# Spreading the softmax reciprocals over the channels: a float32 product of four rows becomes a float16 product of eight rows

## What is computed

```
qkv = (xs @ w_proj.T + b_proj).reshape(B, H * W, N_HEADS, 3 * D_K)
q, k, v = split(qkv)                        # 4 heads, D_K = 16, 784 tokens
attn = softmax(einsum('bihk,bjhk->bijh', q, k) * D_K**0.5, axis=2)
h = einsum('bjhk,bijh->bihk', v, attn)      # weighted values
h = h.reshape(B, H*W, 64) @ w_out.T + b_out
h = h * sigmoid(h) + xs
```

## Time and profile before

| what | value |
|---|---|
| median of 3 runs | 1832.68 us (1827.34 to 1839.15) |
| the profiled execution, its own time | 1829.92 us |
| its span, first to last instruction | 1828.1 us |
| mean granted clock of TensorE | 0.949 of full speed |
| PE busy | 1663.0 us, 91% of the span |
| DVE busy | 1285.1 us, 70% |
| ACT busy | 1022.2 us, 56% |
| POOL busy | 434.1 us, 24% |
| share of PE in the chain that ended last | 81% |

### The profile page before, as it was taken

How to read it: one execution, slowest core, us unless ns; L and a number is a source line. 1 busy time by engine, 2 the same in 40 slices (tenths; PEclk the granted TensorE clock), 3 DMA queues, 4 the chain that set the end, 5 groups by cost and what they waited for, 6 DMA issues and landing times.

```text
span 1828.1 us, 35089 instructions
## 1 busy us (share of the span) xinstructions
PE 1663.0 (91%) x10910; PEld 751.8 (41%) x10910; DVE 1285.1 (70%) x2603; ACT 1022.2 (56%) x1401; POOL 434.1 (24%) x333
## 2 busy tenths in 40 slices
PE   0799689997884999999999999999999999999997
PEld 0333245554873244444434434434443443444332
DVE  5677467887784887777767767666776776767762
ACT  0100166674331176777767667666676776767676
POOL 0400011112102212423413223232341423323111
PEclk9999899999897599999999989989999999999999
DMA  8111166663002332332233322332322332224300
GB/s 197 41 51 45 40 108 100 109 102 54 0 0 33 50 43 33 48 58 43 35 48 50 49 43 33 47 51 46 48 33 43 53 53 43 33 47 54 47 11 19
DMA packets 70267, 93.31 MB, mean 51 GB/s; under 512 B 22648, under 2 KB 63224, under 8 KB 69968
## 3 DMA queue, kind: packets, MB, share of 16 engines
q1 hardware_dynamic: 67728, 89.59, 29.9%
q0 software_dynamic: 2368, 1.57, 1.0%
HBM read 9.00 MB, written 6.42 MB: 8 GB/s over the span
## 4 chain that ended last, share of the span: by engine, by line
PE 81%; DVE 6%; ACT 4%; DMA 3%; SPq 3%; issue 3%; DVEq 0%; POOL 0%; ACTq 0%; POOLq 0%
PE ps L1051 20%; PE ps L1041 18%; PE ps L986 16%; PE ps L861 8%; PE ps L885 5%; PE ps L900 3%; PE ps L1032 3%; PE ps L1007 2%; ACT arena L679 2%; DMA x<-x_in 2%; PE ps L947 2%; SPq L433 2%; PE ps L1024 1%; DVE arena L1430 1%; PE ps L1015 1%
## 5 line engine op out<-in xcount | busy, mean ns | idle before, releaser
L1430 DVE TENSOR_REDUCE arena<-ps 128x1 f32<-128x392 f32 x1600 | 827.0, 559 | 329.5 <-PE ps L986 316.1
L792 ACT ACTIVATE arena<-ps 112x784 f32<-112x784 f32 x896 | 703.4, 822 | 270.4 <-PE ps L1041 265.8
L986 PE MATMUL ps<-arena 112*128 112x392 bf16 x1536 | 491.1, 348 | 8.7 <-DMA arena<-arena 8.2
L1041 PE MATMUL ps<-arena 114*112 114x392 bf16 x1792 | 457.1, 342 | 19.9 <-issue 14.8
L1051 PE MATMUL ps<-arena 112*32 112x392 f32 x3584 | 401.2, 520 | 0.4 <-ACT arena L792 0.4
L986 PEld LDWEIGHTS ps<-arena 112*128 112x128 bf16 x1536 | 151.2, 99 | 377.4 <-DVE arena L1430 307.5
L1041 PEld LDWEIGHTS ps<-arena 114*112 114x112 bf16 x1792 | 230.2, 136 | 140.7 <-issue 50.8
L885 PE MATMUL ps<-arena 96*128 96x392 f16 x768 | 142.2, 336 | 22.0 <-DMA arena<-arena 16.5
L679 ACT ACTIVATE arena<-ps,magic,arena 128x784 f32<-128x784 f32 x128 | 128.2, 1004 | 37.2 <-PE ps L885 37.0
L861 PE MATMUL ps<-arena 128*64 128x392 f32 (+1 forms) x768 | 139.5, 505 | 3.9 <-DMA arena<-arena 3.9
L1051 PEld LDWEIGHTS ps<-arena 112*32 112x32 f32 x3584 | 71.3, 109 | 147.7 <-issue 146.0
(11 more groups left out here) (139 smaller groups left out, 1381.9 us busy)
## 6 DMA issues: line engine op xcount, KB each, us to landing
arena<-arena SPq DMA_DIRECT2D x504, 73.5 KB, 2.7
arena<-arena SPq DMA_DIRECT2D x256, 84.2 KB, 2.8
x<-x_in SPq DMA_DIRECT2D x8, 784.0 KB, 21.2
out<-x SPq DMA_DIRECT2D x16, 392.0 KB, 2.4
arena<-arena SPq DMA_DIRECT2D x252, 24.5 KB, 2.3
arena<-arena SPq DMA_DIRECT2D x256, 1.5 KB
arena<-arena SPq DMA_DIRECT2D x16, 225.0 KB, 3.4
arena<-arena SPq DMA_DIRECT2D x16, 224.8 KB, 2.9
```

Of the source, the lines that this page charges most:

```text
L792: nc.scalar.activation(probs[w % 2][:, 2 * pair:2 * pair + 2, :], two(2 * place, rows=slice(0, TT)), ACT.Exp).then_inc(s_taken, 1)
L986: last = nc.tensor.matmul(ps[:, bank, 0:CH], q[0:ROWS_L, h, it * 128:(it + 1) * 128], k[0:ROWS_L, h, c * CH:(c + 1) * CH], start=True, sto ...
L1041: last = nc.tensor.matmul(ps[0:TT, 2 * place + j, 0:CH], ks[s % 4][0:ROWS_ALL, h, jt * TT:(jt + 1) * TT], qs[s % 4][0:ROWS_ALL, h, c * CH: ...
L1430: nc.vector.tensor_reduce(mx[img % 2][:, c, v:v + 1], scores, AX.X, ALU.max).then_inc(s_mf, 1)
```

## The change

DVE makes two float16 numbers of every reciprocal, times 1024: the rounded value, and what the rounding left. `gather` sends them as two transfers to eight rows. The stationary matrix becomes 8 x 128 float16 with entries 1/1024, so that the product adds the high and the low part again. It is cast once, ahead of the attention's first token.

```diff
+RECIP_UNIT = 1024.0
...
-        den_row = part([NH, T])
+        den_parts = part([NH * DEN_ROWS, 2, T // DEN_ROWS], F16)
+        den_row = part([2 * NH, T], F16)
+        head_rows = part([2 * NH, 128], F16)
...
             def gather(n):
                 wait_apart(pool, s_recip, n)
-                pool.dma_start(den_row[:, :], den_packed[:, :]).then_inc(s_row, 16)
+                for k in range(2):
+                    pool.dma_start(den_row[k * NH:(k + 1) * NH, :], den_parts[:, k, :]).then_inc(s_row, 16)
...
-                    last = nc.tensor.matmul(ps[:, 2 * place + c, 0:CH], P("head_rows", NH),
+                    last = nc.tensor.matmul(ps[:, 2 * place + c, 0:CH], head_rows[:, :],
                                             den_row[:, c * CH:(c + 1) * CH], start=True, stop=True)
...
                     if what == "den":
-                        pe.wait_ge(s_row, lin(lambda t: 16 * t, s, i, 4))
+                        pe.wait_ge(s_row, lin(lambda t: 32 * t, s, i, 4))
...
             v.tensor_scalar(q_bias[:, :], P("bq"), DK**0.5, None, ALU.mult)
+            link(v.tensor_copy(head_rows[:, :], P("head_rows", 2 * NH)))
...
             def reciprocals(n16):
                 dve.wait_ge(s_packed, n16)
-                v.reciprocal(den_packed[:, :], den_packed[:, :]).then_inc(s_recip, 1)
+                link(v.reciprocal(den_packed[:, :], den_packed[:, :]))
+                link(v.tensor_scalar(den_parts[:, 0, :], den_packed[:, :], RECIP_UNIT, None, ALU.mult))
+                v.scalar_tensor_tensor(den_parts[:, 1, :], den_packed[:, :], RECIP_UNIT, den_parts[:, 0, :],
+                                       ALU.mult, ALU.subtract).then_inc(s_recip, 1)
```

More of the change, by code:

```diff
@@ L1504, in _ @@
             v.tensor_tensor(xp(NP - 1), xp(NP - 1), gate[:, :], ALU.add).then_inc(s_done, 1)
-LINKS3 = 4 * 1
+LINKS3 = 4 * 3
 def pack(a):
@@ L1556, in pack @@
     put("b_out", np.tile(a["L3_conv_b_out"], 2)[:, None])
-    put("head_rows", np.kron(np.eye(NH, dtype=f), np.ones((1, 2 * DK), f)), slice(0, NH))
+    rows = np.kron(np.eye(NH, dtype=f), np.full((1, 2 * DK), 1.0 / RECIP_UNIT, f))
+    put("head_rows", np.concatenate([rows, rows]), slice(0, 2 * NH))
     w0 = a["L0_conv_weight"].transpose(1, 0, 3, 4, 2).reshape(C, W0_COLS)
```

## The result

The changed kernel takes 1788.4 us (median of 4 runs, 1786.88 to 1790.92), the kernel before 1833.28 us in the same comparison (4 runs, 1827.34 to 1839.15): 0.976 times as long, 95% interval 0.972 to 0.979. The profiled execution took 1786.88 us at a mean granted clock of 0.963. Against the 1829.92 us of the profiled execution before that is 43.0 us less; 44.1 less were forecast (1785.8, given as 1786 us).

The account below looks back on a forecast made before the run. PE's queue was taken to bound the attention, with low-clock stretches behind "den" adding time. 1829.9 - 23.0 (queue) - 21.4 (clock) + 0.3 = 1785.8, given as 1786 us; range 1773 to 1812 us.

Parts of the forecast that it names:

- the queue of the attention: PE's work and waits around "den": 0.85 us less in 15 even steps, 0.64 in 16 odd ones, together 23.0 us.
- the clock: 17 stretches of PE at 1.2 GHz behind "den" go, 1.26 us each, 21.4 us; bounds nothing and 29 us.
- ahead of the attention's first reciprocal: One chained cast of the matrix ahead of the first token: 0.2 us, taken as 0.25.
- The exponential's wait: The unit after "den" needs the place ACT's exponential frees, so starts at least 1.47 us after the unit before.
- The pitch of the product: On PE the float16 "den" product was taken at 0.17 us, one instruction each; float32 cost 1.56 us extra per entry.
- The 0.04 us: Gain per entry because the first score product behind a float32 one takes 0.21 us to its second instead of 0.17.
- DVE's chain: Three small DVE instructions make reductions 0.5 us later, delaying PE 0.5 us in odd steps and 0.28 in even ones.
- The gather: POOL's second transfer, issued 0.70 us later, makes PE wait 0.45 us in even steps, covered by the exponential; none in odd.
- The 1.26 us: Price of one low-clock stretch, from differences between loop rounds of 149.33, 152.95 and 154.58 us.
- the clock stays: Rival: the low-clock stretches have another cause or the new idle time brings them too; 1807 us, chance 0.19.
- The gather's second transfer sets the start of "den": Rival: 4.0 us from issue to landing; even steps lose 0.53 us, odd ones stay; 1817 us, chance 0.11.
- run one behind the other: Rival: the gather's two transfers are serial, the second there 5.68 us after the first issue; 1861 us, chance 0.04.

Follow-up runs that it names:

- experiment 2: Kernel before with the float16 product of four rows and one transfer, the low part of the reciprocals left out: 1775.58 us, ratio 0.968.
- experiment 5: Changed kernel with its float16 product over 128 rows, the 120 added ones holding ones with zero weights: 1785.8 us, ratio 0.976.
- experiment 3: Kernel before with its float32 product over 128 rows instead of four, the added rows meeting zero weights: 1791.49 us, ratio 0.977.
- experiment 6: Changed kernel with the output store of odd steps issued ahead of the 24 copies of q and k: 1783.77 us, ratio 0.974.
- experiment 4: Changed kernel with each float16 product of eight rows issued five times: 1877.24 us, ratio 1.022 to the kernel before.
- experiment 1: Kernel before, float32 product kept, plus the two chained DVE instructions and a second transfer that PE waits for: 1852.62 us, ratio 1.008.
- experiment 11: Changed kernel, store first, odd-step "den" behind unit 25 instead of 24, odd-step reciprocals at unit 20 instead of 18: 1792.16 us, ratio 0.976.

## Why the prediction was right

The mechanism held: the queue on PE sets the pace, the exponential of the unit before sets what an entry can gain, and the 17 stretches at 0.50 go. That the total came so close (1785.8 us forecast, 1786.88 in the profiled execution, 1788.4 the median) is luck, for its terms were off by more, in both directions. From one profiled execution to the other, read off the timelines:

| part | forecast, us | measured, us |
|---|---|---|
| the queue of the attention | -23.0 | -16.5 |
| the clock | -21.4 | -29.5 |
| ahead of the attention's first reciprocal | +0.3 | +3.2 |
| idle in the gaps between rounds | 0 | -0.3 |
| sum | -44.1 | -43.1 |

**The queue.** The entries are 27.2 us shorter from unit to unit. From the reciprocal to the unit of "den" the steps are 10.7 us longer, 7.6 in odd and 3.1 in even ones. That leaves 16.5 us: 9.3 in odd steps, where 10.2 were forecast, and 7.2 in even ones, where 12.8 were. The missing part is the gather.
- *The exponential's wait* held to 0.02 us: 1.49 us in odd steps and in unhindered even ones, against 1.47 forecast. It stays at 1.49 with one transfer (experiment 2) and with 128 rows (experiment 5).
- *The pitch of the product* was mis-sized: 0.27 us where 0.17 was taken from the wide float16 products of the second layer. It cost nothing, as experiment 5 shows, because the exponential ends later. What the prediction charged to the float32 form (1.56 us for an entry) is in part a matter of four rows: 0.58 us (experiment 3).
- *The 0.04 us* for a faster pair of score products behind "den" did not come: the pair still shows 0.54 us. It was 1.2 us of the 23.0.
- *DVE's chain* was right: 0.67 us to the next reduction against 0.24 before, so 0.43 us where 0.5 was forecast, and it reaches PE as 0.51 us in odd steps and 0.21 in even ones, where 0.28 was forecast.
- *The gather.* The term was wrong in size and in its cause. Forecast were 0.45 us in every even step, hidden behind the exponential; measured are 0.55 to 0.85 us in nine of fifteen and at most 0.1 in six, since without a disturbance "den" can start 2.5 us behind the second issue and not 2.84. The step that failed is "SP's copies of them are for images that PE reaches in the next step, some 20 us on, and cost nothing". The copies do cost nothing here; but the output's store stands behind them in SP's queue. Before, it went out 0.30 us behind the reciprocal and ahead of the gather, now 1.60 us behind it and on top of the gather. Of these 1.30 us 0.72 come from POOL's second issue and DVE's chain, which push the parts of k, the copies and the store back. The other 0.58 come from PE: its steps are shorter, so the next reciprocal comes 23.03 us behind the one of the odd step instead of 23.61, while SP's copies take as long as before. In experiments 2 and 3, which have neither chain nor second issue, the store moves too, to 1.0 to 2.1 and 0.6 to 1.0 us behind the reciprocal in seven of the eight even steps in question. Experiment 6 takes the store away and eight of the nine waits go or shrink, for some 5 us.

**The clock.** Forecast 21.4 us for 17 stretches; all 17 are gone, and two pieces of 3.4 us behind the gaps as well, which nobody forecast. The price of one was mis-sized. The same piece of a step, with a stretch in it and without, 124 products of PE each:

```profile
1601.55:1619.73 18.18, 18.18 (x124) 8.65 (x124) 11.52 (x22) 12.34 (x20) 2.62 (x3) 0.91 0.60 86
1450.69:1467.29 16.60, 16.60 (x124) 8.13 (x124) 11.37 (x23) 12.24 (x20) 2.64 (x3) 1.00 0.61 82
```

That is 1.58 us, and over all pieces 1.55 us each: 26.4 us for the 17 and 3.1 for the two. The 1.26 us came from rounds of the loop that end in gaps of different length:

```profile
1530.36 0.87 PE L1041 MATMUL ps<-arena 114*112 114x392 bf16 x4 [3.68 <-issue]
...
1381.03 1.18 PE L1041 MATMUL ps<-arena 114*112 114x392 bf16 x3 [2.55 <-issue]
...
1228.08 1.22 PE L1041 MATMUL ps<-arena 114*112 114x392 bf16 x3 [2.53 <-issue]
```

The round taken as the one with least clock loss holds 1.1 us more idle time than the other two, and each difference was too small by as much.

That a long product of few rows stands before the fall, and not float32 or an idle gap, is now shown: float32 over 128 rows has none behind it (experiment 3), the short float16 product over four or eight rows none (2 and the change), and eight rows five times over bring them back (4), in odd steps without a wait of PE. The rival "the clock stays" is out, though PE now idles in front of "den". In the Trainium skill, "TensorE: Matmul & The Clock Gate", section "Why this matters for your kernels", the lower clock comes from idle gaps between bursts; the stretches behind the loop's gaps agree with it, the 17 before and those in the odd steps of experiment 4, with PE busy ahead of the fall, don't. What it is in a product of few rows that the chip answers to is not shown here.

**Ahead of the attention.** The first reciprocal comes 3.2 us later than before. The change has no more than the cast there, and over all profiled executions of this document that point lies anywhere from 686.7 to 692.3 us, so this is the spread of the layers ahead and no effect of the change.

**The other rivals.** *The gather's second transfer sets the start of "den"* came true in the nine even steps, with a landing after 3.1 to 3.4 us in eight of them instead of 4.0, so that these entries still gained 0.25 to 0.55 us. A landing over 3 us was named as a sign of being wrong, and for this term it was one. The two transfers don't run one behind the other: each lands 2.4 us after its own issue (median), though the issues are 0.7 us apart. The product is cheaper: 62 instructions of 335 ns.

## What to carry to other kernels

A matrix product with a few rows of weights is not cheap: compare it with the same product over all 128 rows before changing its type. Follow every queue behind a delayed instruction to its last entry, and also where the engines around it become faster; the copies that were free had a 392 KB store behind them. Before a stretch of time is priced from two pieces of a trace, compare what else they hold, their idle gaps above all. And where a ring of two places is fed by one engine and drained by another, moving a short entry by one unit moves the wait, and may lay it on top of the next one.

## What the runs showed of the hardware

- A float32 product of four rows by 392 columns costs 0.28 us more than one over 128 rows (1.11 against 0.83 us from one `max_chunk` to the next, experiment 3); a float16 one of eight rows 0.54 us, with a pitch of 0.27 us to either neighbour, where the same product over 128 rows has 0.17 (experiment 5). Among themselves the products of eight rows follow at 0.17 us too (experiment 4).
- The granted clock fell to 0.50 (1.2 GHz), mostly for 3.4 us at a time, behind long products of few rows: 17 times in 31 before, with no idle time of PE in the 3.4 us ahead of any; 19 times in experiment 1 and 25 in experiment 4, where 13 and 15 had none ahead; and never behind the same float32 product over 128 rows. Each 3.4 us cost some 1.55 us.
- Transfers of 6 KB land 2.4 us after their issue (median), and in the changed kernel up to 3.4 us where a store of 392 KB runs beside them (350 GB/s in the window above). A store is not needed for it: in experiment 11 the second of them took up to 3.5 us beside the last copies of q and k (86 GB/s over the 3.4 us behind the issue at 1446.14).
